# One stage of a transformer block on one core: TensorE's written-out rounds become a hardware loop

## The reference

```python
gate = jnp.einsum('btd,edi->beti', x, Wg)
up = jnp.einsum('btd,edi->beti', x, Wu)
h = jax.nn.silu(gate) * up
e_out = jnp.einsum('beti,eid->betd', h, Wd)
out = jnp.einsum('bte,betd->btd', weights, e_out)
...
x = x + _L1_ffn_ref(_layernorm(x, axis=-1), L1_ffn_Wg, L1_ffn_Wu, L1_ffn_Wd, L1_ffn_Wr, L1_ffn_temperature)
```

## Time and profile before

| | |
|---|---|
| median of three runs | 2557.96 us (2557.19 to 2559.76) |
| profiled execution | 2557.19 us, of which span 2555.7 us |
| PE busy | 2285.4 us (89%), 14663 matmuls |
| DVE, ACT, POOL busy | 1524.9, 814.4, 463.4 us |
| PE's instruction packets (queue q8) | 79, 1.29 MB in the whole span |
| the stage changed | about 1450 us to the end |

### The profile page before, as it was taken

One profiled execution on the slowest core, in us unless ns is written; L12 is line 12 of the kernel. 1 busy time (PEld: TensorE's weight loads), 2 busy tenths in 40 slices (PEclk: granted clock), 3 DMA queues, 4 the chain that ended last, 5 costly groups with the idle time before them and its releaser, 6 DMA issues. The chain is left out here.

```text
span 2555.7 us, 39481 instructions
## 1 busy us (share of the span) xinstructions
PE 2285.4 (89%) x14663; PEld 1958.7 (77%) x14663; DVE 1524.9 (60%) x3239; ACT 814.4 (32%) x1098; POOL 463.4 (18%) x413
## 2 busy tenths in 40 slices
PE   5888888665799985999999599999999999999999
PEld 3677777543688874777777488888888888888888
DVE  4788787476455536777777476545454544545454
ACT  1343434212444421433433252222222222222222
POOL 3122222010665633222222130000000000000000
PEclk8999999875899997999999799999999999999999
DMA  2021211110444431111111310000000000000000
GB/s 70 27 69 54 66 57 50 51 34 0 122 96 95 69 36 33 64 60 49 57 62 38 115 50 26 25 26 26 25 25 25 25 25 25 25 25 25 18 11 15
DMA packets 117498, 114.85 MB, mean 45 GB/s; under 512 B 15440, under 2 KB 114320, under 8 KB 117392
## 3 DMA queue, kind: packets, MB, share of 16 engines
q1 hardware_dynamic: 105104, 96.29, 11.9%
q0 software_dynamic: 12288, 17.05, 4.1%
HBM read 62.72 MB, written 50.59 MB: 44 GB/s over the span
## 5 line engine op out<-in xcount | busy, mean ns | idle before, releaser
L1795 DVE TENSOR_TENSOR zmix_hid<-zmix_act_gate,psum 128x1024 f32<-128x1024 f32 x128 | 156.3, 1221 | 389.6 <-issue 359.3
L143 PE MATMUL psum<-zmix_wd_hi,zmix_hid_hi 128*128 128x256 f32 x1024 | 289.3, 283 | 1.9 <-DVE zmix_acc L1786 1.7
L145 PE MATMUL psum<-zmix_wd_hi,zmix_hid_lo 128*128 128x256 f32 x1024 | 289.8, 283 | 0.0
L144 PE MATMUL psum<-zmix_wd_lo,zmix_hid_hi 128*128 128x256 f32 x1024 | 289.7, 283 | 0.0
L1739 ACT ACTIVATE zmix_act_gate<-psum 128x1024 f32<-128x1024 f32 x128 | 131.7, 1029 | 403.7 <-PE psum L145 403.7
L1747 ACT ACTIVATE zmix_hid_hi<-zmix_hid 128x1024 fp32r<-128x1024 f32 x128 | 135.5, 1059 | 383.5 <-PE psum L145 285.8
L594 PEld LDWEIGHTS psum<-att_v_cur,att_probs 128*128 128x128 f32 x2048 | 248.3, 192 | 9.7 <-ACT att_probs L694 3.6
L594 PE MATMUL psum<-att_v_cur,att_probs 128*128 128x96 f32 x2048 | 245.5, 273 | 2.7 <-ACT att_probs L694 2.7
L1800 DVE TENSOR_TENSOR zmix_hid_lo<-zmix_hid,zmix_hid_hi 128x1024 fp32r<-128x1024 f32 x128 | 158.7, 1240 | 135.1 <-ACT zmix_hid_hi L1747 134.2
L143 PE MATMUL psum<-zmix_xT_hi,zmix_wg_hi 128*128 128x512 f32 x512 | 203.2, 397 | 12.2 <-DVE zmix_xT_lo L1775 12.2
L1786 DVE SCALAR_TENSOR_TENSOR zmix_acc<-psum,zmix_weight,zmix_acc 128x256 f32<-128x256 f32 x512 | 211.7, 476 | 1.6 <-PE psum L145 1.6
(11 more groups left out here) (284 smaller groups left out, 4768.2 us busy)
## 6 DMA issues: line engine op xcount, KB each, us to landing
x<-att_x_new SPq DMA_DIRECT2D x32, 512.0 KB, 2.9
att_x_in<-in_x SPq DMA_DIRECT2D x16, 512.0 KB, 3.9
rows<-att_normed_new SPq DMA_DIRECT2D x16, 512.0 KB, 3.0
att_x_in<-x SPq DMA_DIRECT2D x16, 512.0 KB, 3.9
normed<-att_normed_new SPq DMA_DIRECT2D x16, 512.0 KB, 2.9
zmix_xn<-normed SPq DMA_DIRECT2D x16, 512.0 KB, 4.7
zmix_acc<-x SPq DMA_DIRECT2D x16, 512.0 KB, 4.3
out_x<-zmix_acc SPq DMA_DIRECT2D x16, 512.0 KB, 3.2
```

Of the source, the lines that this page charges most:

```text
L143: pe.matmul(out, st_hi, mv_hi, start=first, stop=False)
L144: pe.matmul(out, st_hi, mv_lo, start=False, stop=False)
L145: return pe.matmul(out, st_lo, mv_hi, start=False, stop=last)
L1795: dve.tensor_tensor(hid[:, :, :], act_gate[:, :, :], psum[:, 2:4, :], ALU.mult).then_inc(up_out, 1)
```

## The change

PE's Python loop over rounds 1 to 6 becomes a hardware loop over the same rounds. The program of PE then holds rounds 0, one general round and round 7. In the general round r is a register value, and so are b, n and all semaphore values made of them. The other engines' programs stay as they are.

```diff
             turn(0, 0, 0)
             gate_up(0, 0, 0, True)
             steps(0, False, True)
-            for r in range(1, LAST):
+            with pe.Fori(1, LAST) as r:
                 steps(r, False, False)
             steps(LAST, True, False)
```

## The result

The changed kernel takes 2586.08 us (median of 4 runs, 2585.46 to 2589.61) against 2557.57 us before: 1.0113 times as long, 95% interval 1.0096 to 1.0131. It is slower by 28.5 us, and outside the range of the forecast.

The account below looks back on a forecast made before the run. PE was taken as the bound, busy 135.00 of 135.00 us a round. From 2557.19 us, 0 each for fetch, register work, branches and missing head gave 2557.2, stated as 2558.0 to match the runs' median; range 2554.5 to 2564.

Parts of the forecast that it names:

- Fetching less code: PE's zone-mixture rounds: about 37 fewer instruction packets, some 45 in place of 79, gaining 0 us.
- Register work and branch: PE's sequencer in the zone-mixture loop: 86 register operations a round and five jumps back, hidden by its lead, costing 0.
- Rival B: Register work shows because the sequencer is late at the zone mixture's downs: 3.5 us, 2561.5 us; chance 0.06.
- Rival C: Zone mixture's 256-column matmuls start 113 ns apart instead of 120 without code streaming: 16 us back, 2542 us; chance 0.03.
- Whether the code is still there: At PE's jumps back: the loop touches 7 blocks, at worst 8, all taken as kept; cost 0.
- Rival A: PE's loop head is not kept, so jumps back must fetch it: 2562.5 to 2572 us; chance 0.18.
- The price of a missing head: If PE's loop head is gone: 0.9 to 2.8 us a back edge, 14 us far end for five; taken as 0.

Follow-up runs that it names:

- e1: Changed kernel with the loop's first instruction placed at the start of a 256-instruction block; 2558.23 us median, ratio 1.0004 to the kernel before.
- e2: Changed kernel with the loop's first instruction at place 160 of a block, code over 7 blocks; 2549.9 us in one execution.
- e4: Changed kernel with a hint at the loop's top announcing the jump back, head left in place; 2556.88 us median, ratio 1.0002 to the kernel before.
- e3: Changed kernel with the loop's first instruction at place 192 of a block, last instructions in an eighth block; 2564.18 us in one execution.
- e5: Changed kernel with the loop's first instruction at place 224, 32 instructions ahead of the next block, over 8 blocks; 2568.05 us in one execution.
- e6: Changed kernel with the loop's first instruction at place 239, 17 instructions ahead of the next block, over 8 blocks; 2574.91 us in one execution.
- e7: Changed kernel with two rounds in the loop's body, three passes, two back edges, no hint; 2571.4 us in one execution.

## Why the prediction was wrong

**Fetching less code: right that it gives nothing, wrong in count.** PE is no faster in e1, where no packet comes for 700 us. But the changed kernel fetched nine blocks in each of rounds 2 to 6. A sum in the prediction is wrong too: six rounds of 6.3 blocks that become one of 6.6 are 31 packets fewer, not "about 37", and 48 are left, not "some 45". 48 is what e1, e2 and e4 have.

**Register work and branch: 0, right.** In e1, with both, batches are 67.62 us apart. Rival B's 3.5 us did not appear. The count was too high: between two branches of e1 (1746.8 to 1882.0 us) there are 40 register operations where 86 were forecast, and one separate wait in place of 20. The round has 1610 instructions, not 1680; from a head this close to the end of its block both lie over eight blocks.

**Rival C: wrong.** In e1 the matmuls of 256 columns still start 0.12 us apart while nothing is fetched, for instance at 1748.45, 1748.57 and 1748.69:

```profile
1748.45 0.28 PE L143 MATMUL psum<-zmix_wd_hi,zmix_hid_hi 128*128 128x256 f32 x1
1748.57 0.28 PE L144 MATMUL psum<-zmix_wd_lo,zmix_hid_hi 128*128 128x256 f32 x1
1748.69 0.28 PE L145 MATMUL psum<-zmix_wd_hi,zmix_hid_lo 128*128 128x256 f32 x1
```

**Whether the code is still there: this step failed,** in the sentence "so a block begins within some ten or twenty instructions of the loop's head; the loop then touches 7 blocks, at worst 8". The boundary was where I had read it, but just behind the head and not just before it. A reading good to ten or twenty instructions could not tell the two sides apart, and they are 7 and 8 blocks. Nor did I add the block fetched ahead to the loop's own: 8 + 1. Rival A named this mechanism and got 0.18; the gap that it foretold near 1744 us came, with nine packets a round and not "six or seven".

**The price of a missing head: the size of one fetch right, the rest missing.** The sum had 0 here and 14 us as the far end; the five back edges cost 28.75. "0.9 to 2.8 us a back edge" holds for e3 and e5, which lost 1.6 to 2.1 us; the branch that has to fetch takes 3.3 to 3.9 us on the sequencer, less the lead of 1.9 us of the earlier trace rows. What failed is "The blocks behind the head would stream in as they do before, at no cost." With the boundary about six instructions behind the head, the next block is asked for when the matmuls issued ahead are used up. The first matmul behind the second wait starts 3.0 to 3.5 us after the end of the branch, and two matmuls are all that lies before it. That is the gap of 2.1 to 2.6 us. Third, I had no term for the clock. Of the 28.75 us, 7.0 + 11.2 are shown as waits; most of the other 10.5 is the half clock: about 40 matmuls at 0.43 instead of 0.23 us, 8 us. This share is read from the rows; no run has these gaps at the full clock throughout. At the ten back edges of e3 and e5, with one gap each, the clock did not fall, in e6 it fell at one of five, in the changed kernel and in e7 at all seven. Why it fell at that one of e6 stays open.

The Trainium skill, page "Runtime: NRT & Kernel Launch", section "Instruction fetch mechanics", gives PE room for 2048 instructions. That is eight blocks, and e4 agrees: a loop over eight is kept. Its warning that a jump out of a window of two pages has to fetch was right about the changed kernel's loss, but two is not the number here: e1 and e2 jump back over seven blocks with branches of 208 ns.

## What to carry to other kernels

Before a written-out program becomes a hardware loop, count its blocks from where the head will lie, and add the one fetched ahead; a loop just under the room can fail by the place of its head alone, and an edit anywhere ahead of it moves that place. If it doesn't fit, or is near, announce the jump or fix the head's place; both cost nothing here and both only restored the old time, because PE's written-out code had been fetched for free. The lead of the sequencer (1.9 us here) is what a jump may cost unseen; a second stop right behind the first finds it used up.

## What the runs showed of the hardware

A branch whose target had to be fetched kept PE's sequencer 3.3 to 3.9 us, though the packet moved for about 1 us. The placement of the head made 0, 9, 16 or 29 us of difference by the distances of the batches, with the same instructions in the loop. PE kept eight blocks when the ninth was not fetched ahead, and with nine in turn it kept none of them: every block was fetched again in each round. At the changed kernel's first back edge the granted clock fell behind 4.9 us in which PE had worked 0.95. It was 0.50 for 3.4 us (1749.4 to 1752.8), and at the third back edge for 6.8 us (2029.3 to 2036.1).
